# A decoder layer on one core: head scores in four row groups of TensorE, wider products for V, a series by products, and all queues in a new order

## The reference, cut to what matters

```python
# part 1: attention on 64 latent keys, 16 heads of 16 values, the 4 largest scores alone
Q = x @ Wq.T + bq;  V = x @ Wv.T + bv
logits = einsum('bhtd,lhd->bhtl', Q, latent) / sqrt(16)
top, idx = top_k(logits, 4);  weighted = softmax(top) @ latent[idx]
x = layernorm(x + (weighted + V) @ Wo.T + bo)
# part 2: cross attention, 16 heads, rotary context of 64 rows
q_r = (((x @ Wq.T) per head) @ w_kc_q) @ W_qr;  k_r = kv_rope @ W_kr
attn = softmax(q_r @ k_r.T)                       # over 64 rows of context
x = layernorm(x + ((attn @ kv_rope) @ w_kc_kv) @ Wo.T)
# part 3: gated unit of 1024, inputs rounded to 8 bits, ternary weights
wq = round(tanh(w / (s + eps))) * arctanh(s),  s = mean(abs(w))
h = silu(quant(x) @ wq1.T) * (quant(x) @ wq2.T);  x = layernorm(x + quant(h) @ wq3.T)
```

## Time and profile before

| | us |
|---|---|
| median of three runs | 349.58 |
| the profiled execution, its own time | 349.29 |
| span of its instructions | 347.6 |
| PE busy | 330.5 (95%) |
| DVE busy | 287.0 (83%) |
| ACT busy | 281.4 (81%) |
| POOL busy | 251.9 (72%) |
| granted TensorE clock | 0.999 of full speed over the span |

### The profile page before, as it was taken

How to read it: one execution, slowest core, us unless ns; L and a number is a source line. 1 busy time by engine, 2 the same in 40 slices (tenths; PEclk the granted TensorE clock), 3 DMA queues, 4 the chain that set the end, 5 groups by cost and what they waited for, 6 DMA issues and landing times.

```text
span 347.6 us, 7479 instructions
## 1 busy us (share of the span) xinstructions
PE 330.5 (95%) x2539; PEld 243.4 (70%) x2539; DVE 287.0 (83%) x718; ACT 281.4 (81%) x535; POOL 251.9 (72%) x228
## 2 busy tenths in 40 slices
PE   8999999999789899999999999999999999999893
PEld 4767776787567676787777767777778777666341
DVE  2667296999599999898789999999889877998882
ACT  2857899886479399888988898988987988999783
POOL 3357536999889698898658888779749757577561
PEclk9999999999999999999999999999999999999999
DMA  7999700000000000000000000000000000000001
GB/s 224 414 412 417 270 0 2 0 4 2 0 0 3 1 2 0 17 0 4 15 2 17 16 3 1 17 0 18 2 0 18 15 3 15 15 2 16 18 16 45
DMA packets 5653, 17.58 MB, mean 51 GB/s; under 512 B 624, under 2 KB 3056, under 8 KB 4720
## 3 DMA queue, kind: packets, MB, share of 16 engines
q1 hardware_dynamic: 5616, 17.12, 12.9%
HBM read 15.02 MB, written 2.10 MB: 49 GB/s over the span
## 4 chain that ended last, share of the span: by engine, by line
PE 60%; DVE 18%; POOL 10%; issue 8%; ACT 3%; POOLq 0%; DVEq 0%; ACTq 0%
PE wide L524 9%; PE small L562 8%; PE wide L583 5%; PE wide L508 4%; PE wide L445 3%; PE small L432 3%; PE wide L457 3%; PE small L480 3%; PE small L606 3%; PE small L484 3%; PE wide L539 3%; PE wide L550 2%; DVE m L1073 2%; PE small L469 2%; PE wide L355 2%
## 5 line engine op out<-in xcount | busy, mean ns | idle before, releaser
L562 PE MATMUL small<-V_sb,PT_sb 128*128 128x256 f32 x256 | 58.5, 381 | 1.3 <-DVE y_row L1104 1.3
L562 PEld LDWEIGHTS small<-V_sb,PT_sb 128*128 128x128 f32 x256 | 47.7, 190 | 8.9 <-DVE y_row L1104 1.5
L1339 POOL TENSOR_TENSOR Ls<-Ls,m 128x1024 f32<-128x1024 f32 x16 | 32.3, 2019 | 29.0 <-DVE mask L1087 29.0
L524 PE MATMUL wide<-B_sb,x1T 128*128 128x512 f32 x192 | 49.6, 407 | 0.0
L1073 DVE MAX8 m<-Ls 128x8 f32<-128x64 f32 x256 | 33.9, 210 | 11.5 <-ACT Ls L774 10.4
L1402 POOL TENSOR_TENSOR region_c<-region_c,region_q 128x1024 f32<-128x1024 f32 (+1 forms) x17 | 32.3, 1902 | 13.8 <-DVE region_c L1197 11.6
L524 PEld LDWEIGHTS wide<-B_sb,x1T 128*128 128x128 f32 x192 | 35.4, 188 | 9.8 <-issue 1.2
L1354 POOL TENSOR_TENSOR Ls<-Ls,mask 128x1024 f32<-128x1024 f32 x16 | 37.8, 2365 | 1.3 <-ACT Ls L787 0.5
L1377 POOL TENSOR_TENSOR P<-P,r 128x1024 f32<-128x1024 f32 x16 | 32.6, 2036 | 6.8 <-DVE r L1141 6.8
L1346 POOL TENSOR_TENSOR mask<-mask,r 128x1024 f32<-128x1024 f32 x16 | 30.4, 1902 | 8.0 <-DVE r L1096 6.9
L583 PE MATMUL wide<-tern,region_k 128*128 128x512 bf16 x128 | 32.1, 379 | 0.7 <-ACT region_k L888 0.6
(11 more groups left out here) (184 smaller groups left out, 868.7 us busy)
## 6 DMA issues: line engine op xcount, KB each, us to landing
region_q<-in_wqx SPq DMA_DIRECT2D x1, 2048.0 KB, 16.7
region_c<-in_woTx SPq DMA_DIRECT2D x1, 2048.0 KB, 8.5
out_x<-region_q SPq DMA_DIRECT2D x16, 128.0 KB, 1.7
first<-in_xT SPq DMA_DIRECT2D x7, 256.0 KB, 9.9
region_c<-in_wkcqT SPq DMA_DIRECT2D x1, 1536.0 KB, 11.6
region_r<-in_wqkr SPq DMA_DIRECT2D x1, 1024.0 KB, 7.5
region_r<-in_w1T SPq DMA_DIRECT2D x1, 1024.0 KB, 11.0
region_t<-in_w2T SPq DMA_DIRECT2D x1, 1024.0 KB, 12.8
```

The source lines that it names most:

```text
L524: mm = pe.matmul(ps_L2[:, r * 512:(r + 1) * 512], x1T[:, u, k, :], B_sb[:, s, w, k, r * 512:(r + 1) * 512], start=(u == w == k == 0), stop ...
L562: mm = pe.matmul(ps_O2[:, 0:D], PT2_sb[:, c, :], V_sb[:, c, :], start=(c == 0), stop=(c == PAIRS - 1))
L1339: pool.tensor_tensor(heads(Ls[n % 2][:]), heads(Ls[n % 2][:]), over_heads(m8[:, :, 0:1]), ALU.subtract).then_inc(g_d1, 1)
```

## The change

Five things change.

1. `L1` takes 32 rows of the array in a product (2 heads, 128 columns), 8 products in all, four after another in the four row groups of the array, each into its own bank: two in `wide1`, two in `wide2`. `copy_L1` reads as many values as before, with two instructions, each from two banks. `lat_k` is half as wide, and made by three small operations instead of four.
2. `V_` makes 4 products of 512 columns instead of 8 of 256.
3. `T2_` does four products of one kind (u) before it changes to the other.
4. The series on POOL is made by products: the square of the mean, then twice, four and eight terms by multiplication; no power operation.
5. Places in PSUM move (`T1_`, `T2T`, `S3`, `C_`, the last tile's `Z_` and `HT`), and the order of all four engines is written anew. `warm` has 50 products.

```diff
-        ps_L1 = wide[1]
+        ps_L1 = (wide[1], wide[2])
-        ps_C = (wide[0], wide[2])
+        ps_C = (wide[2], wide[2])
...
             def T2_(*freed):
-                for i in range(PAIRS):
+                for i in range(PAIRS // 2):
                     for u in range(2):
-                        for e in range(2):
-                            c = (i + e * PAIRS // 2) % PAIRS
+                        for e, c in ((0, i), (1, i + PAIRS // 2), (1, i), (0, i + PAIRS // 2)):
...
             def L1(n, *freed):
-                bank_of(*freed)
+                for k in range(0, len(freed), 2):
+                    bank_of(*freed[k:k + 2])
...
                 for g in range(KD):
-                    for j in range(2):
-                        mm = pe.matmul(ps_L1[:, j * 512 + g * SEQ:j * 512 + (g + 1) * SEQ],
-                                       QT[b % QRING][j * L:(j + 1) * L, g, q * P:(q + 1) * P],
-                                       lat_k[j * L:(j + 1) * L, g, :], start=True, stop=True)
+                    for j in range(4):
+                        rows = slice(32 * j, 32 * (j + 1))
+                        col = (j % 2) * 512 + g * 2 * L
+                        mm = pe.matmul(ps_L1[j // 2][:, col:col + 2 * L],
+                                       QT[b % QRING][rows, g, q * P:(q + 1) * P], lat_k[rows, g, :],
+                                       start=True, stop=True)
...
             def V_(half, b, *freed):
-                for c in range(2):
+                for e in range(2):
                     for r in range(2):
                         rows = slice(r * L, (r + 1) * L)
-                        for e in range(2):
-                            mm = pe.matmul(ps_V[half][e * L:(e + 1) * L,
-                                                      r * 512 + c * D:r * 512 + (c + 1) * D],
-                                           kv[rows, b, :], C_sb[rows, 2 * half + c, e, :],
-                                           start=True, stop=True)
+                        mm = pe.matmul(ps_V[half][e * L:(e + 1) * L, r * 512:(r + 1) * 512], kv[rows, b, :],
+                                       C_sb[rows, 2 * half:2 * half + 2, e, :], start=True, stop=True)
...
             def atanh_series():
-                link(pool.tensor_tensor(terms[:], mean.rearrange("p (w o) -> p w o", o=1)
-                                        .to_broadcast([P, 3, TERMS]), exponents, ALU.pow))
-                link(pool.tensor_tensor(terms[:], terms[:], coefs, ALU.mult))
+                link(pool.tensor_tensor(square, mean, mean, ALU.mult))
+                link(pool.tensor_tensor(terms[:, 0], mean, square, ALU.mult))
+                for k in (1, 2, 4):
+                    link(pool.tensor_tensor(terms[:, k:2 * k], terms[:, 0:k], prep[:, 6:7, :]
+                                            .to_broadcast([P, k, 3]), ALU.mult))
+                    if k < 4:
+                        link(pool.tensor_tensor(square, square, square, ALU.mult))
+                link(pool.tensor_tensor(terms[:], terms[:], series.rearrange("p (k o) -> p k o", o=1)
+                                        .to_broadcast([P, TERMS, 3]), ALU.mult))
...
-            Z_(1, 4, None, a_L1, 13); HT(3, None, v_y2, 7); PT2(7, v_bl, 12); V_(1, 4, v_g1, 5)
+            Z_(1, 4, None, v_bl, 11); HT(3, None, v_y2, 7); L2(8, a_PT2, 8); XQT(5, a_Q, 8)
+            L1(12, v_g2, 5, v_g1, 5); O2(7, a_hT, 4); V_(1, 4, a_L1, 13); O3(3, a_qT, 6)
```

More of the change, by code:

```diff
@@ L88, in decoder_layer @@
         prep = sb("prep", [P, 11, 3])
-        terms = sb("terms", [P, 3, TERMS])
+        terms = sb("terms", [P, TERMS, 3])
         atanh_q = sb("atanh_q", [P, 3])
@@ L200, in decoder_layer @@
         ps_T2 = wide[0]
-        ps_T2T = wide[2]
+        ps_T2T = wide[1]
         ps_WF = small[0]
         ps_WB = small[1]
-        ps_S3 = small[0]
+        ps_S3 = small[1]
         ps_Z = (wide[2], wide[1])
@@ L207, in decoder_layer @@
         ps_V = (wide[2], wide[2])
-        ps_T1 = (wide[2], wide[0])
+        ps_T1 = (wide[0], wide[1])
         ps_A = (wide[0], wide[2])
-        ps_C = (wide[0], wide[2])
-        ps_Z_last = (wide[1], wide[0])
-        ps_HT_last = (wide[1], small[0])
+        ps_C = (wide[2], wide[2])
+        ps_L1 = (wide[1], wide[2])
+        ps_Z_last = (wide[0], wide[1])
+        ps_HT_last = (wide[0], wide[2])
         def low_halves(ap):
@@ L677, in _ @@
-            HT(15, 0, v_g1, 17); HT(15, 1, a_hT, 15); warm(2, wide[0], p_warm, 9)
+            warm(9, wide[0]); Q(0); warm(4, wide[0], p_warm, 1); L1(0); T1_(0, p_warm, 2)
+            T1_(1, a_L1, 1); Q(1, a_Q, 1); L1(1, a_T1, 2, a_L1, 1); T2_(a_T1, 1); WF()
+            L1(2, a_L1, 2, a_L1, 2); PT1(0, a_T2k, 1); Q(2, a_Q, 2); T2T(a_L1, 3)
+            WT(0, v_WF, 1); WB(a_Q, 3); A_(0, a_PT1, 1); A_(1, a_L1, 3); B_(0, 0, a_T2, 1)
+            PT1(1, a_A, 1); O1(0, a_AT, 1); L1(3, v_bl, 1, a_A, 2); Q(3, v_WB, 1)
@@ L772, in copy_L1 @@
                 since(act, p_PT1, n - 1)
-                for j in range(2):
+                for half in range(2):
                     ins = act.activation(
-                        Ls[n % 2][:].rearrange("p (g j n) -> p j g n", g=KD, j=2)[:, j],
-                        ps_L1[:, j * 512:(j + 1) * 512].rearrange("p (g n) -> p g n", g=KD), ACT.Copy)
+                        Ls[n % 2][:].rearrange("p (g h j n) -> p h g j n", g=KD, h=2, j=2)[:, half],
+                        ps_L1[half][:].rearrange("p (j y g n) -> p y g j n", j=2, y=2, g=KD)[:, 0], ACT.Copy)
                 ins.then_inc(a_L1, 1)
@@ L1294, in _ @@
             mean, one_m, ratio, ln_in, ln_out = (prep[:, k, :] for k in (1, 2, 3, 4, 5))
-            acc, small = (prep[:, k, :] for k in (7, 10))
+            square, acc, small = (prep[:, k, :] for k in (6, 7, 10))
             chain = [0]
@@ new lines, in _ @@
+            root_1(1); weights_1(3); shift_1(4); scale_mask(4); ratio_of_means(); root_1(2)
+            weights_2(0); weights_1(4); shift_1(5); root_1(3); scale_mask(5); weights_1(5)
+            weights_2(1); root_2(0); shift_1(6); gain_x(0); root_1(4); scale_mask(6)
+            weights_1(6); root_1(5); atanh_series(); roots_x(0); atanh_weights(); root_2(1)
+            weights_2(2); shift_1(7); weights_2(3); gain_x(1); scale_mask(7); weights_1(7)
+            root_1(6); roots_x(1); root_2(2); gain_h(0); roots_h(0); gain_x(2); shift_1(8)
@@ new lines, in _ @@
+            roots_x(2); scale_mask(8); weights_1(8); root_2(3); weights_2(4); root_3(0)
+            root_1(7); gain_h(1); gain_x(3); roots_x(3); roots_h(1); weights_2(5); shift_1(9)
+            scale_mask(9); weights_1(9); weights_2(6); root_2(4); gain_x(4); root_3(1)
+            roots_h(2); root_1(8); roots_x(4); gain_h(2); shift_1(10); scale_mask(10)
+            weights_1(10); root_2(5); root_1(9); gain_x(5); gain_h(3); roots_h(3); weights_2(7)
+            shift_1(11); root_3(2); root_2(6); root_1(10); roots_x(5); scale_mask(11); gain_h(4)
@@ new lines, in _ @@
+            roots_x(6); roots_h(4); weights_1(11); gain_x(6); shift_1(12); scale_mask(12)
+            weights_1(12); root_2(7); gain_h(5); weights_2(8); root_3(3); gain_x(7); root_1(11)
+            roots_x(7); shift_1(13); roots_h(5); scale_mask(13); weights_2(9); root_1(12)
+            weights_1(13); root_2(8); root_3(4); shift_1(14); gain_h(6); roots_h(6)
+            scale_mask(14); roots_x(8); gain_x(8); weights_1(14); weights_2(10); root_3(5)
+            root_2(9); gain_h(7); shift_1(15); root_1(13); gain_x(9); roots_x(9); weights_2(11)
@@ new lines, in _ @@
+            scale_mask(15); roots_h(7); weights_1(15); root_3(6); gain_h(8); root_1(14)
+            root_2(10); gain_x(10); weights_2(12); roots_h(8); roots_x(10); root_3(7)
+            root_2(11); gain_x(11); gain_h(9); roots_x(11); weights_2(13); roots_h(9); root_3(8)
+            root_2(12); root_1(15); weights_2(14); gain_h(10); gain_x(12); roots_h(10)
+            roots_x(12); root_2(13); root_3(9); gain_h(11); gain_x(13); roots_h(11); roots_x(13)
+            weights_2(15); root_2(14); root_3(10); gain_h(12); roots_h(12); gain_x(14)
@@ L1468, in rope_tables @@
+            roots_x(14); root_2(15); gain_h(13); roots_h(13); root_3(11); gain_x(15)
+            roots_x(15); gain_h(14); roots_h(14); root_3(12); gain_h(15, 0); gain_h(15, 1)
+            roots_h(15); root_3(13); root_3(14); root_3(15)
 def rope_tables():
```

407 lines of the change are left out of this document (186 added, 221 removed).

## The result

The changed kernel took 350.17 us in the median of 20 runs (349.83 to 353.39), the kernel before 349.55 beside it (20 runs). That is slower by 0.6 us, where 340.5 was forecast. The ratio, which takes in every run, is 1.0036 (95% interval 1.0018 to 1.0053), or 1.3 us: 14 of the 20 runs took 349.83 to 350.35, and six took 351.50 to 353.39, at granted clocks of 0.986 to 0.995. The profiled execution took 350.15, at a clock of 1.000.

A forecast was written before the change was run, and what follows sets the result against it. PE was taken to bound 140 to 284 us, with three engines waiting for each other before. 349.3 less 4.6 (`L1`), 1.2 (`T2_`), 0.3 (`V_`) and 3.0 (series) gave 340.2, as a median 340.5 us; range 336.5 to 345.5.

The forecast's parts named there:

- the new order of the tail: Steps behind the last `L1`: new order taken to cost nothing, bound 1.1 us each way, one copy of a tile's scores.
- The slower rival: `L1`'s scores hold `wide1` and `wide2` until copied; about 1.1 us at each of 11 calls, 12 us, 352.5; chance 0.12.
- `L1`: PE, four row groups: 0.64 us a call, 0.42 saved, 11 calls on the chain, 4.6 us.
- The estimate of about 0.8 us for a call: `L1` on PE, by the skill's 3.07 times for four row groups: about 0.8 us a call, sum 342.
- `T2_` and `V_`: PE: `T2_` saves 1.2 us by fewer changes between kinds of product, `V_` 0.3 us by fewer records and loads.
- The series: POOL: twelve small operations replace 7.65 us, 3.4 to 4.4 us after; with DVE's idle time, 3.0 us gained, bounds 0 and 3.7.
- The bound of 4.4 us: Series on POOL: takes 4.4 us instead of 3.4 if the operation on 24 elements keeps its 1.26 us.
- The sum: Whole kernel: 349.3 - 4.6 - 1.2 - 0.3 - 3.0 = 340.2; the median 0.3 above, 340.5 us.
- The upper end of the forecast's range: Whole kernel: 345.5 us, from half of `L1`'s gain and a third of the series'.
- The four-loads rival: `L1` on PE: four loads go two at a time, a call stays at 1.06 to 1.09 us, total 345; chance 0.08.
- the order is worth more: PE's idle time from 60 to 140 and behind 284 us: the order removes a third, total 335; chance 0.12.
- DVE takes it back: DVE where PE is the bound: its steps come late for PE, most of the gain goes, 349; chance 0.08.

The follow-up runs named there:

- the order alone: Old instructions of all parts (50 products of zeros) in the changed kernel's order and PSUM places, no wait for `wide2`: 354.46 us, ratio 1.0149 to the kernel before.
- third and fourth orders: Single steps moved on four engines: all four parts 346.60 and 345.98 us (third with three zero products 346.03); without new `L1` 345.12 and 344.86 us.

## Why the prediction was wrong

349.5 + 5.0 (the order alone) - 4.3 (all parts in it) = 350.2. The forecast had 0 and 9.1.

- **The order: this step failed.** "I cost the new order of the tail at nothing; its bound is the length of one copy of a tile's scores each way", and for the stretches ahead the only rival made the order worth more. The order alone costs 5.0 us, 2.7 of it ahead of `L2(15)`, and 2.4 behind, where DVE comes with 3.0 us more to do. The order of the tail itself makes 0.6 of it. All four parts with the same hold take 346.6 and 346.0 in other orders, 3.6 and 4.2 us less than here, so this isn't the cheapest order that the hold allows; how much of the 5.0 the hold forces isn't shown.
- **The slower rival** was out for the changed kernel: 0.7 us of waits at `L1`, and taking the hold away changes nothing (353.76 against 353.62). Its cause is real elsewhere. In the old order the hold makes 15.0 us of waits at `L1` and 20.8 at the steps that want `wide1` or `wide2` next, three times the rival's 12. The earlier trace rows couldn't show this; the order of the steps could have, by asking which step of the old order needs `wide2` while the scores stand there.
- **`L1`**: 0.66 us a call as forecast, worth 3.4 us for 4.6 with the other parts in place (11 calls of 0.42; 3.4 us are 8 calls). The estimate of about 0.8 us for a call doesn't follow from the factor that it names: the 1.86 us of 16 records one by one, over that factor, are 0.61, and 0.66 is 2.8 times faster than one by one.
- **`T2_` and `V_`**: 1.4 us for 1.5, in the old order. Right.
- **The series**: 3.0 forecast, 2.9 in the new order beside all the other parts, 0.2 in the old one (against its own runs of before, 349.66). The 1.26 us that the earlier trace rows have for the multiplication are not its own: it takes 0.23 where DVE leaves it alone. The bound of 4.4 us "if it keeps its 1.26" took a wait for a length.
- **The sum** treated the parts as links of one chain. The series is POOL's and DVE's, `L1` is PE's, and with either one as before the time is 353 to 354 (353.04, 353.76): the second gain only comes with the first. The upper end of the forecast's range was added up loosely too: half of `L1`'s gain and a third of the series' give 344.8 with the 1.2 of `T2_`, and 345.5 only with its lower bound of 0.5.
- **The four-loads rival** and "the order is worth more" are out: 0.66 us a call, and +5.0. "DVE takes it back" (349) was nearest in time, but by luck: DVE does come late with 3.0 us of work at `L2(15)`, and it does so with the old parts too, by the order and not by a faster PE.

What stays open: which single moves of the change's order cost the 2.7 us ahead of `L2(15)`, what the hold alone costs in the third and fourth orders, and whether it is DVE's remaining work that lengthens the tail. `L1` in four row groups within one wide tensor wasn't tried: two row groups would write to one bank at a time.

## What to carry to other kernels

An order written anew has a price of its own, which no length of a step shows: run the old parts in the new order before you believe the sum of the parts. A part that needs one more buffer for as long as another engine copies can cost nothing or far more than it saves, by what stands behind it (0 us in the change's order, some 36 us of waits in the old one). Gains on different engines don't simply add: 3.4 and 2.9, each on top of the rest, were 4.3 for all parts together. And a length read from one row, for an operation that another engine can hold up, is to be compared with its shortest like before it enters a sum.
